# A time-mix recurrence with 32-column products: sharing a loaded operand, and who turns the results

## What is computed

```python
def step(S, inp):
    r_, w_, k_, v_, kk_, b_ = inp
    sab = jnp.einsum('bhvk,bhk->bhv', S, kk_)
    S = S * jnp.exp(w_)[:, :, None, :] + sab[..., None] * b_[:, :, None, :] + v_[..., None] * k_[:, :, None, :]
    y = jnp.einsum('bhvk,bhk->bhv', S, r_)
    return (S, y)
```

## Time and profile before

| what | us |
|---|---|
| median of 3 runs | 7474.48 |
| the profiled execution | 7475.47 |
| its span, first to last instruction | 7473.7 |
| mixer, from the start to about | 5500 |
| experts, the rest | 1970 |

### The profile page before, as it was taken

One profiled execution on the slowest core, in us unless ns is written; L12 is line 12 of the kernel. 1 busy time (PEld: TensorE's weight loads), 2 busy tenths in 40 slices (PEclk: granted clock), 3 DMA queues, 4 the chain that ended last, 5 costly groups with the idle time before them and its releaser, 6 DMA issues. The chain is left out here.

```text
span 7473.7 us, 335127 instructions
## 1 busy us (share of the span) xinstructions
PE 6255.1 (84%) x156232; PEld 4507.1 (60%) x156232; DVE 3933.7 (53%) x9069; ACT 1922.3 (26%) x3659; POOL 1468.3 (20%) x1284
## 2 busy tenths in 40 slices
PE   5887888878778888888888788787748999999999
PEld 5666666667666666666666666666634444444444
DVE  5666666666666666666666666666533322323210
ACT  3333333333333333333333323333210000000000
POOL 1212112221111211222121211212102121122120
PEclk8999999989999999999999999999958999999999
DMA  1000000000000000000000000000011122112120
GB/s 49 20 15 15 15 18 18 15 15 15 18 18 15 15 15 18 18 15 15 17 19 15 15 15 16 19 15 15 11 63 44 60 80 81 51 58 69 64 79 11
DMA packets 108970, 216.92 MB, mean 29 GB/s; under 512 B 25424, under 2 KB 26704, under 8 KB 107088
## 3 DMA queue, kind: packets, MB, share of 16 engines
q1 hardware_dynamic: 92240, 144.98, 6.6%
q0 software_dynamic: 15360, 50.48, 2.0%
HBM read 144.67 MB, written 50.72 MB: 26 GB/s over the span
## 5 line engine op out<-in xcount | busy, mean ns | idle before, releaser
L367 DVE COPY_PREDICATED time_raw<-time_known,w_bank 128x96 f32<-128x96 int32 (+6 forms) x3072 | 834.9, 273 | 482.7 <-PE w_bank L849 401.1
L1668 PE MATMUL moe_bank<-moe_w,moe_hidden 128*128 128x512 f32 x2048 | 928.7, 596 | 0.0
L1655 PE MATMUL moe_bank<-moe_hT,moe_w 128*128 128x512 f32 x2048 | 924.7, 594 | 0.8 <-DVE moe_hT L1555 0.8
L1655 PEld LDWEIGHTS moe_bank<-moe_hT,moe_w 128*128 128x128 f32 x2048 | 386.8, 191 | 472.2 <-issue 471.0
L1668 PEld LDWEIGHTS moe_bank<-moe_w,moe_hidden 128*128 128x128 f32 x2048 | 379.4, 190 | 429.5 <-issue 428.1
L1576 ACT ACTIVATE moe_hidden<-moe_bank,moe_b 128x512 f32<-128x512 f32 x256 | 175.9, 687 | 1628.1 <-PE moe_bank L1655 1628.1
L849 PE MATMUL w_bank<-time_keys,time_queries_u 128*128 128x160 f32 x2048 | 423.4, 358 | 172.5 <-DVE time_bonus L462 165.5
L781 POOL TENSOR_TENSOR time_tail<-time_tail,time_lp 128x512 f32<-128x512 f32 x64 | 75.6, 1181 | 2163.7 <-ACT time_lp L706 2099.7
L749 POOL TENSOR_TENSOR time_queries_u<-time_dq,time_kkn 32x512 f32<-32x512 f32 x256 | 325.9, 1273 | 840.4 <-ACT time_dq L626 825.3
L836 PE MATMUL w_bank<-time_invT,time_part 32*32 32x32 f32 x32768 | 412.4, 198 | 75.9 <-issue 54.6
L849 PEld LDWEIGHTS w_bank<-time_keys,time_queries_u 128*128 128x128 f32 x2048 | 352.6, 227 | 192.2 <-DVE time_bonus L462 172.8
(11 more groups left out here) (235 smaller groups left out, 10580.2 us busy)
## 6 DMA issues: line engine op xcount, KB each, us to landing
moe_w<-in_w SPq DMA_DIRECT2D x64, 1024.0 KB, 7.4
mid_xn<-time_xn_rows SPq DMA_DIRECT2D x128, 129.0 KB, 2.7
time_x_rows<-in_x SPq DMA_DIRECT2D x128, 128.0 KB, 2.7
time_base<-in_x SPq DMA_DIRECT2D x128, 128.0 KB, 3.0
mid_acc<-time_mixed SPq DMA_DIRECT2D x128, 128.0 KB
mid_scores<-time_rated SPq DMA_DIRECT2D x128, 2.0 KB, 1.7
moe_b<-in_b SPq DMA_DIRECT2D x8, 256.0 KB, 12.6
time_receptance<-in_w_receptance SPq DMA_DIRECT2D x1, 1024.0 KB, 4.8
```

The lines of the kernel that those rows point to most:

```text
L367: e.copy_predicated(by_raw[:, "uy".index(q), n0:n1, :, 0:8 * j + 8], known[:, "uy".index(q), :, :, mine].to_broadcast([P, n1 - n0, 2, 8 * ...
L1655: got = e.matmul(up[now % 3][:, :], w1[:, g * F + k * P:g * F + (k + 1) * P], hT[x % 2][:, g * CAP + half * HALF:g * CAP + (half + 1) * HA ...
L1668: got = e.matmul(down[t][:, :], hidden[now % 4][:, t * P:(t + 1) * P], tile(w2, k), start=k == 0, stop=k == FC - 1)
```

## The change

**Products.** The groups of a chunk become four, so that products with the same operand loaded are one. `from_values` loads a block of vT and passes 96 columns: uk, yk and kT. `from_state` loads the state and passes 64: us and ys. `u_of` stays. `from_solved` loads corr and passes 64: yb and bT. All three sums, z, y and s, stand in one tensor `sums` over banks 6 and 7, four columns of blocks in each bank, in the order z, y, s in even turns and s, z, y in odd ones, so that kT and bT of both turns can lie beside the turned scores (`by_values`, `by_solved`, `by_state`). The solved block moves to bank 2.

**Turning.** z and s now come out turned. VectorE turns z into `rhs` (`turn_z`) where ScalarE copied it, and turns s into `grown` before it scales it (`C.rows`). y is copied by ScalarE as before, after `C.rows`.

**Moved.** On VectorE, uk is turned behind the bonus, yb and yk before the u4 masks, and the last level of the inverse (T3) stands before the new pairs. On TensorE, the last two parts of value stand later, the bonus product behind both halves of P1, delta3 alone behind low_wa, the scores y1 and y3 one place earlier. On ScalarE, the copy of P0 stands before the mix tanh, that of v behind N.rstd, that of the first solved block before A.lp.

```diff
+        COLUMNS = ({"z": 0, "y": N, "s": 2 * N}, {"s": 0, "z": N, "y": 2 * N})
+        passed = lambda t, q0, q1, n, h: t[h * N:(h + 1) * N, :].rearrange("p (q n t) -> p n q t", n=U, t=N)[:, n, q0:q1]
...
+        both_banks = ctx.enter_context(nc.psum_tensor("w_bank67", [P, 1024], F32))
+        sums = both_banks[:, :].rearrange("p (n q t) -> p n q t", n=SU, t=N)
...
-            ("P3", 6, act, "C.P3"), ("solve.z0", 6, act, "C.z0"), ("solve.s0", 6, dve, "C.shrunk0"),
+            ("P3", 6, act, "C.P3"), ("sums0", 6, act, "C.y0"), ("sums1", 6, act, "C.y1"), ("Q0", 7, dve, "C.T0"), ("Q1", 7, dve, "C.T1"),
...
+            def turn_z(c):
+                e.wait_ge(pe.sem, pe[f"C.z{c}"])
+                e.transpose(chunks(rhs), sums[:, :, at["z"] // N]).then_inc(dve.sem, dve.step(f"C.z{c}"))
+
             def state_of(c):
-                e.wait_ge(pe.sem, pe[f"C.s{c}"])
-                e.tensor_tensor(chunks(grown), wide(BANK[f"solve.s{c}"][:, 0:SU * N]), per_su(got["shrink"], c), ALU.mult).then_inc(
+                e.wait_ge(pe.sem, pe[f"C.y{c}"])
+                e.transpose(chunks(grown), sums[:, :, at["s"] // N]).then_inc(dve.sem, dve.step(f"C.rows{c}"))
+                e.wait_ge(dve.sem, dve[f"C.rows{c}"])
+                e.tensor_tensor(chunks(grown), chunks(grown), per_su(got["shrink"], c), ALU.mult).then_inc(
                     dve.sem, dve.step(f"C.shrunk{c}"))
                 e.wait_ge(dve.sem, dve[f"C.shrunk{c}"])
                 e.wait_ge(pool.sem, pool[f"C.faded{c}"])
-                e.wait_ge(pe.sem, pe[f"C.y{c}"])
...
             if Cs:
-                solved("z", 0)
+                solved("u", 0)
...
+            def from_values(c):
+                clear(e, f"sums{c}")
+                clear(e, f"more{c}")
                 if c == 0:
+                    e.wait_ge(dve.sem, dve["C.T3"])
                     e.wait_ge(dve.sem, dve["C.yk"])
+                q0 = 1 - turn % 2
                 for su in range(SU):
                     for h in range(HG):
+                        e.matmul(sums[head(h), su, 0:3], got["vT"][head(h), blk(su * NC + c)],
+                                 passed(by_values, q0, q0 + 3, su * NC + c, h), start=su % 4 == 0, stop=False,
+                                 skip_group_check=True)
...
+            def from_state(c):
...
+                        mm = e.matmul(sums[head(h), su, q0:q0 + 2], state[head(h), blk(su)],
+                                      passed(by_state[turn % 2], 0, 2, su * NC + c, h), start=False, stop=False,
+                                      skip_group_check=True)
...
+            def from_solved(c):
+                e.wait_ge(act.sem, act[f"C.u{c}"])
...
+                        mm = e.matmul(sums[head(h), su, 1:3] if turn % 2 == 0 else sums[head(h), su, 0:3:2],
+                                      corr[head(h), blk(su)], passed(by_solved, q0, q0 + 2, su * NC + c, h),
+                                      start=False, stop=True, skip_group_check=True)
...
+                clear(e, "delta3")
+                delta_of(3).then_inc(pe.sem, pe.step("A.delta3"))
```

More of the change, by code:

```diff
@@ L1002, in on_tensor @@
             if Bs:
+                value_of(3, 4).then_inc(pe.sem, pe.step("B.value"))
+            if Cs:
+                P_of(1, 1)
+            if Bs:
                 clear(e, "bonus")
```

175 lines of the change are left out of this document (70 added, 105 removed), and 12 rows, old and new, of the table DVE_STEPS.

## The result

The changed kernel takes **6798.09 us** (median of 4 runs, 6791.71 to 6802.26) against 7473.74 us of the kernel before beside it: ratio 0.9102, with 0.9084 to 0.912 as its 95% interval. The forecast was 7041, with 6855 as its lower end: the direction was right, the size a third too small (434 us forecast, 676 measured).

A forecast was written before the change was run, and what follows sets the result against it. TensorE was taken as the engine to follow, busy 68.6 of 84.6 us a turn. Terms -2.0 + 1.1 - 2.5 - 1.9 - 1.7 = -7.0 us, times 62 turns, gave 7041 us from 7475, range 6855 to 7230.

The forecast's parts named there:

- Issue gaps: TensorE idle with nothing shown as waited for: halving the recurrence's 4.3 us gives -1.9 us a turn, ends 0 and -4.3.
- Products: Recurrence's eight groups a chunk become four: 1.0 us less a chunk, -2.0 us a turn, ends -1.4 and -5.5.
- first rival: Merged groups cost hardly more than narrow ones: -4 instead of -2.0 us a turn, about 6915 us, chance 0.15.
- Fourth delta: Delta product alone behind low_wa on TensorE, other three still about 1.1 us: +1.1 us a turn, possibly +0.8.
- Waits: TensorE's waits for other engines fall from 9.0 to 6.45 us: -2.5 us a turn, ends -5 and +0.5.
- the walk: One turn followed on both engines at row prices: VectorE some 1.2 us late for last sums, mix waits 1.15 us.
- the 2.57 us before the first u score: TensorE's wait for the bonus product, claimed to go whole as uk, yb, yk leave and the delta product fills 1.1 us.
- the early copy: ScalarE's solved-block copy ahead of lp, lns, rs, rs2: removes the state product's wait, -1.63 us a turn.
- Clock: TensorE's 4.2 us a turn excess from low clock after gaps shrinks: -1.7 us a turn, ends 0 and -3.5.
- The ends worked out first: Terms' far ends combined by root of summed squares: about 5.2 us a turn towards faster, 4.0 towards slower.
- second rival: VectorE's order becomes the bound, z turns holding it: waits rise 5 us, -2.0 us a turn, 7350 us, chance 0.13.
- The third: Packed tiles stop running side by side at 64 or 96 columns: 60 to 90 ns a MATMUL, about 8240 us, chance 0.03.

The follow-up runs named there:

- e3: Changed kernel with VectorE's transposes of uk, yb and yk put back between xf1 and the keys: 6809.95 us, ratio 0.9116.
- e10: Changed kernel with TensorE's head of the turn (value parts, bonus product, four deltas together) and ScalarE's copies of P0 and v in old order: 6982.2 us, ratio 0.935.
- e4: Changed kernel with ScalarE's copy of the first solved block put back behind lp, lns, rs and rs2: 6823.52 us, ratio 0.9135.
- e8: Changed kernel with VectorE's turn of the second z moved behind wmk, g1, p2 and fk: 6676.05 us, ratio 0.8936.

## Why the prediction was wrong, step by step

**Issue gaps: the step that failed.** "Halving these gives -2.1; as fewer gaps here can mean more elsewhere I take -1.9. Ends 0 and -4.3." Measured 7.0 - 1.6 = -5.4 us a turn, beyond its far end. The gaps were read as a property of dense lines, and only those on the recurrence's lines were taken to be at stake. They belong to blocks of 256 instructions in program order: with 512 MATMULs taken from the turn's end, the blocks there last long enough for the next to come. Not half of the recurrence's 4.3 us went but all of it, and with it the 1.0 us on the line of the projections, which share its blocks. Only the gaps elsewhere stayed, 1.6 us. Of the 3.2 us a turn by which the forecast was short, this step is 3.5. What could have shown it blind was in the trace: counting the MATMULs between two gap ends.

**Products:** -2.0 forecast, 2 x (5.48 - 4.20) = -2.56 measured. The price per column was nearly right for 64 and 96 columns, and slightly too high. The first rival (width is free) is false: 1.03 us against 0.69 for the same 64 MATMULs. The Trainium skill, "TensorEngine Tiling (Array Packing)", section "Instruction Overhead", gives one column and 60 the same latency: the rate of this packed stream doesn't follow that from 32 to 64 columns. The latency of a single MATMUL, of which the page speaks, no run here shows.

**Fourth delta:** +1.1 forecast; delta3 alone takes 1.09 to 1.21 us and the other three still 1.10. Right.

**Waits:** -2.5 forecast, 7.5 - 9.0 = -1.5 measured. By place: mix 1.15 forecast and 2.2 measured (107.4/48.4), low_wa 1.75 and 1.3, low_k with P2 1.25 and 1.3, y4 0.7 and 0.9, the loop's head 1.1 and 0.8, the copy before Q3 0.5 and 0.2, the solved block 0 and 0. The places named were right. One that the forecast doesn't have is P0's wait for ScalarE's copy of y, which now stands behind VectorE's turning of s: 23.1/48.4 = 0.5. Mix was nearly twice the forecast, and the walk had the lateness right (1.2 us forecast, 1.28 seen). What it had too small is the scaling product, 0.35 us against 1.33 beside GpSimd; that alone is nearly the whole miss there. The turning took 0.44 us, not 0.35. Of the reasons, one was wrong: "the 2.57 us before the first u score **go whole**" since three transposes leave. The wait did go (1.2 us in all 48 turns), but e3 and e10 show that TensorE's order did it. The credit for the early copy was too large as well (e4).

**Clock:** -1.7 forecast. Busy time fell by 3.6, of which -2.56 + 1.1 is work: -2.1 for the clock. The size is near, but it is what is left over, no run isolates it, and it was forecast with far fewer gaps gone. The mean granted clock rose from 0.940 to 0.949.

**Sum:** -2.56 + 1.1 - 1.5 - 5.4 - 2.1 = -10.5 a turn, against 10.2 from the transposes. The ends worked out first (5.2 us towards faster) would have held this; the 3 us either way that were used in their place were a judgement with no row behind it. The second rival (VectorE's order the bound) had the right place and not the size: e8 shows 1.9 us a turn at stake there. The third is false, for 64 MATMULs of 64 columns in 1.03 us are 16 ns each.

## What to carry to other kernels

Where "issue" gaps stand in a stream of small MATMULs, count the instructions from the end of one gap to the end of the next before giving them to a line. If the count is constant, the price of an instruction is that of its block: here no block between two gaps took less than 3.3 us, however little was in it. Then merging small products in the densest block pays several times their own time (520 us here, where the products' own was 1.2 us a turn), while spreading them paid a fifth of it (112 us), and taking waits away nearly nothing before the merging (18 us) and 202 us behind it. And take an instruction away from a queue only after asking what its absence moves beside another engine's traffic.

## What the runs showed of the hardware

- **Instructions come to TensorE in blocks of 256, one each 3.3 us at best; half of those that end in a gap take over 3.7.** A block of 128 MATMULs with their loads that runs 2.46 us is followed by a gap of 1.01 us. The turn of before has 2347 x 2 / 256 = 18.3 blocks, 64 us of fetching at 3.5 us in a turn of 84.6: the supply suffices in the mean, and a store of several blocks would have hidden the short ones. The trace speaks against such a store: all 297 gaps end 2.2 to 3.1 us behind the start of the last packet, so nothing but that packet was at hand then. What the 1.3 us between a packet's end and the next block's start are, and why a fetch starts 1.05 us behind a block's beginning in one place and 3 us in another, stays open. The Trainium skill, "Runtime: NRT & Kernel Launch", section "Instruction fetch mechanics", states the blocks of 16 KiB, a DMA queue of the sequencer's own, and the next block fetched while one runs. The trace agrees in all three: 16 KB a packet, a queue whose packets fell with TensorE's instructions alone, and a packet that starts 1.05 us behind a block's beginning. The section also calls the crossing mostly hidden and TensorE's memory 2048 instructions, eight blocks, though further on it speaks of only two lines of 16 KiB. Here gaps without a shown cause cost 7.0 us of an 84.6 us turn and stand at such crossings, and the trace doesn't bear out eight blocks held ahead; it fits two.
- **A packed MATMUL pays its width from 32 columns on:** 32, 64 and 96 columns take 10.8, 16 and 23 ns each (64 in 0.69, 1.03 and 1.45 us).
- **GpSimd's products stretch VectorE's two-input products to three times their time.** For 128x256 they take 0.42 us with nothing on GpSimd and 1.32 us where they begin beside its product and lie beside its work to their end (49 turn ends of the changed kernel, 1000 to 4600 us); in e8, where GpSimd is further on, the latter is 0.82. Transposes of 128x512 take 0.67 to 0.71 us either way.
